# Layer normalisations applied on ScalarE as scale and shift, with the shift and three routing steps on GpSimd

## The chip, the cores and the metric

The kernel runs on one core of a Trainium2 chip. The metric is device time in microseconds (us) of one execution. The engines are named as in the profile: PE (TensorE matmul), PEld (its weight load), DVE (VectorE), ACT (ScalarE), POOL (GpSimd), SP (SyncE, which issues DMAs).

## What is computed

A decoder layer with three residual blocks, each followed by a layer normalisation without gain and bias. x is 16 batches of 256 rows of 256, ctx 16 x 77 x 256.

```
def _layernorm(x, axis=-1, eps=1e-05):
    m = jnp.mean(x, axis=axis, keepdims=True)
    v = jnp.var(x, axis=axis, keepdims=True)
    return (x - m) / jnp.sqrt(v + eps)

x = _layernorm(x + self_attention(x, W_qkv, W_out))        # 16 heads, segments of 128 queries, 64 keys each
x = _layernorm(x + cross_attention(x, ctx, Wq, Wk, Wv, Wo, biases))   # 16 heads, 77 keys
x = _layernorm(x + moe(x))
# moe: logits = x @ router_w; expert = argmax(logits); weight = softmax(logits)[expert]
#      weight * (gelu(x @ w1[expert] + b1[expert]) @ w2[expert] + b2[expert]), 14 experts
```

## The kernel before

Everything is fp32. **Part 1** (up to about 500 us) does the two attentions, their normalisations and the routing, batch by batch. **Part 2** sorts the rows by expert through a list in DRAM and runs 45 tiles of 128 rows through the experts; the change doesn't touch it.

Part 1 is a software pipeline of 21 iterations. In iteration i every engine runs through its own table of jobs, PE_ORDER, ACT_ORDER, DVE_ORDER, POOL_ORDER, in the order written there. An entry such as `ln11@2` is job ln, part 11, on batch i - 2. An entry whose batch is outside 0 to 15 is left out. Within an engine nothing overtakes: an instruction that waits holds all behind it. The tables have six rows; row n belongs to softmax unit n. Units 0 and 1 are the two segments of self-attention (1024 columns), units 2 to 5 the four parts of cross-attention (616 columns).

For a unit: PE `scores` (L556, L565) into the banks ps_s; DVE `max` (L934), `less_max` (L945); ACT `exp` (L812); DVE `sum` (L953), `reciprocal` (L965); POOL `scale` (L1210); PE `probT` (two transposes into PSUM, L543); ACT copies each (L792); PE `attend` (L598, L610); ACT `take_o` (L800, L805).

All other results of PE go through the four banks of ps_r. The jobs of PE that use them follow each other as a ring, so each job takes the bank of the job four places earlier and waits until that one has been emptied (`wait_bank`). In row 4 of PE_ORDER the ring goes probT20, probT21, k0, rk0, oa1, q0: **oa1 takes the bank of probT20, and q0 that of probT21**; in row 5 probT30 takes that of rk0.

Each batch has four normalisations of 128 x 256: 10 and 11 after self-attention (halves 0 and 1 of x1), 20 and 21 after cross-attention (x2s). For each, PE projects (`oa0`, `oa1`, `ox0`, `ox1`, L622), DVE adds the residual into a sum (L986), then bn_stats (L993) and bn_aggr (L1002) for mean and variance; POOL adds eps (L1197) and takes the power -0.5 (L1199); DVE subtracts the mean and multiplies by rstd (L1020, `ln`). x1 goes to PE's x1T and the query projection, x2s to x2T, to DRAM and to the router.

The routing of a batch is 12 small DVE operations (`r_max` to `r_place`, 128 x 28 or less), chained on one semaphore: maximum, logits less maximum (L1042, for ACT's exp of the gate), is-maximum, first of them, counts of earlier rows (L1054, L1058), one-hot. PE `rk` turns them into ranks, which DVE copies out of PSUM (L972), masks (`r_pick`, L1069) and sums (`r_place`, L1072). POOL `enter` writes two entries of the batch into the list by indirect DMA (L1286); the next batch's `r_gate` (L1066) waits until these have landed.

Of the kernel before, what the change touches and what calls it, by code (L numbers as in the profile page):

```python
# [6 lines left out]
P = 128  # L7
# [3 lines left out]
ALU = mybir.AluOpType  # L11
# [25 lines left out]
def decoder_layer(nc, x, x_cols, xk_cols, ctx_cols, w_qkv, w_out, wq, bq, wk, bk, wv, bv, wo, bo, router_w, w1, b1, w2,  # L37
# [31 lines left out]
    with ExitStack() as top:  # L69
# [54 lines left out]
        with ExitStack() as part1:  # L124
# [33 lines left out]
            rstd = sb1("rstd", [P, 4])  # L158
            x1 = sb1("x1", [P, TPB, D])
# [17 lines left out]
        with ExitStack() as part2:  # L177
            def sb2(name, shape, dt=F32):
# [59 lines left out]
        taken = {j: signal(f"taken_{j}", n) for j, n in JN.items()}  # L238
# [42 lines left out]
        def exists(b):  # L281
# [21 lines left out]
            sum0@1 r_weigh0@5 reciprocal0@1 max1@1 r_first0@5 less_max1@1 ln20@3 once0@1  # L303
            sum1@1 r_count0@5 reciprocal1@1 max2@2 less_max2@2 r_onehot0@5 ox1@3 stats21@3 mean21@3
            sum2@2 r_count_tile0@5 reciprocal2@2 max3@2 less_max3@2 r_gate_sum0@5 oa0@1 stats10@1 mean10@1
            sum3@2 reciprocal3@2 ln10@1 max4@2 less_max4@2 r_gate0@5 rk0@5 oa1@1 stats11@1 mean11@1
            ln21@3 sum4@2 r_pick0@5 reciprocal4@2 max5@2 less_max5@2 r_place0@5
# [37 lines left out]
        def wait_bank(pe, what, part, b):  # L345
# [269 lines left out]
        def pe_job(pe, job, part, b):  # L615
# [64 lines left out]
            elif job == "rk":  # L680
                pe.wait_ge(routed.sem, routed.at(b, STAGES.index("count_tile")))
# [133 lines left out]
        def act_take(act, job, part, b):  # L815
# [37 lines left out]
            elif job == "rt":  # L853
                wait(act, routed, b - 1, STAGES.index("is_max"))
                last = nc.scalar.copy(logits[:], src[:, 0:TPB * RW].rearrange("p (t e) -> p t e", t=TPB)[:, :, 0:E])
            last.then_inc(taken[job].sem, 1)

        def act_gate_exp(act, b):
# [3 lines left out]
            act.wait_ge(routed.sem, routed.at(b, STAGES.index("less_max")))  # L862
            wait(act, routed, b - 1, STAGES.index("gate_sum"))
# [8 lines left out]
        def act_iteration(act, i):  # L872
            for what, k, lag in in_order(ACT_ORDER):
# [93 lines left out]
        def dve_take(dve, job, part, b):  # L967
# [3 lines left out]
            if job == "rk":  # L971
                nc.vector.tensor_copy(rank[:], src[:, 0:TPB * E].rearrange("p (t e) -> p t e", t=TPB)).then_inc(  # L972
                    taken[job].sem, 1)
                return
# [438 lines left out]
```

## Time and profile before

| | |
|---|---|
| three runs | 716.0, 716.43 (median), 716.88 us |
| the profiled execution | 715.96 us, span of its trace 714.2 us |
| PE busy in the span | 601.3 us (84%) |
| DVE busy | 499.4 us (70%) |
| ACT busy | 347.7 us (49%) |
| POOL busy | 399.3 us (56%) |

In a timeline row stand start, duration, engine, line, operation, out<-in with shapes, how often, and in brackets the engine's idle time before it with what ended it. A row of the chain of waits has start, duration and what the end of the program waited for at that time. A row of busy times by stretch has the stretch, its length, the busy us of PE, PEld, DVE, ACT and POOL (with instruction counts), the granted TensorE clock as a share of full speed, the DMA share and GB/s. A row of one source line has the smallest, median and largest duration in ns. PE is pipelined, so a busy PE is not a PE at its peak.

### The profile page before, as it was taken

Reading aid. Unit: us, or ns where it says so; the run is one execution under the profiler, and the core shown is the slowest. Engines: PE = TensorE matmul, PEld = TensorE weight load, DVE = VectorE, ACT = ScalarE, POOL = GpSimd, SP = SyncE. Lnnn points to the kernel's source line nnn. Section 1 sums busy time; section 2 is a strip of 40 time slices with the busy share of each in tenths; the row PEclk is TensorE's granted clock in tenths of the full one; section 3 lists DMA queues with packets and bytes.
Section 4 is the critical chain, followed back from the end, with each engine's and each line's share of the span. In section 5 each row is a group of like instructions: output and inputs, shape, how many; then the busy total and the mean of one; then the engine's idle time right before and its main releaser. Section 6 shows DMA issues by size and latency. Waiting matters only on the chain.

```text
span 714.2 us, 17657 instructions
## 1 busy us (share of the span) xinstructions
PE 601.3 (84%) x5736; PEld 493.6 (69%) x5736; DVE 499.4 (70%) x1186; ACT 347.7 (49%) x864; POOL 399.3 (56%) x517
## 2 busy tenths in 40 slices
PE   4679889889898898898988988867279999999991
PEld 3457667667676676676766766645149999999991
DVE  2468868887898798887988878764305556655662
ACT  1346555555555555555555645533034554455540
POOL 3334645655575566564755655534334777777753
PEclk9889999999999999999999999987579999999996
DMA  8223133032231330331313101000033333333200
GB/s 275 83 58 92 21 112 110 13 112 78 53 111 32 101 109 14 112 106 26 111 34 98 29 12 32 18 20 16 1 70 77 100 93 90 97 89 106 72 28 1
DMA packets 75882, 50.17 MB, mean 70 GB/s; under 512 B 38918, under 2 KB 69898, under 8 KB 75792
## 3 DMA queue, kind: packets, MB, share of 16 engines
q1 hardware_dynamic: 70448, 40.60, 20.7%
q0 software_dynamic: 5344, 8.44, 4.0%
q8 instruction: 48, 0.79, 0.5%
q14 instruction: 42, 0.34, 0.2%
HBM read 40.54 MB, written 10.60 MB: 72 GB/s over the span
## 4 chain that ended last, share of the span: by engine, by line
PE 40%; POOL 17%; DVE 17%; issue 16%; ACT 5%; DMA 3%; SPq 1%; POOLq 0%; DVEq 0%; ACTq 0%
PE ps_r L622 17%; PE ps_r L543 7%; POOL out L1359 7%; POOL xg L1347 6%; DVE prob L945 5%; DVE mx L934 5%; PE ps_r L610 4%; PE ps_s L565 3%; POOL rs L1367 3%; DVE den L953 3%; ACT prob L812 3%; PE ps_r L652 2%; DMA token_lists<-member,place_i 2%; ACT qxT L848 2%; PE ps_r L670 2%
## 5 line engine op out<-in xcount | busy, mean ns | idle before, releaser
L1210 POOL TENSOR_TENSOR prob<-prob,rden 128x616 f32<-128x616 f32 (+1 forms) x96 | 138.6, 1444 | 160.5 <-DVE rden L965 160.3
L812 ACT ACTIVATE prob<-prob 128x616 f32<-128x616 f32 (+1 forms) x96 | 80.0, 833 | 68.7 <-DVE prob L945 68.7
L953 DVE TENSOR_REDUCE den<-prob 128x8 f32<-128x616 f32 (+1 forms) x96 | 88.7, 924 | 28.2 <-ACT prob L812 28.2
L934 DVE TENSOR_REDUCE mx<-ps_s 128x8 f32<-128x616 f32 (+1 forms) x96 | 87.0, 907 | 25.1 <-PE ps_s L556 22.3
L792 ACT COPY probT<-ps_r 128x512 f32<-128x512 f32 x192 | 83.3, 482 | 32.0 <-PE ps_r L543 32.0
L543 PE MATMUL ps_r<-ident,prob 128*128 128x128 f32 (+1 forms) x576 | 89.8, 296 | 2.7 <-POOL prob L1210 2.7
L945 DVE TENSOR_TENSOR prob<-ps_s,mx 128x616 f32<-128x616 f32 (+1 forms) x96 | 90.2, 940 | 2.5
L757 PEld LDWEIGHTS ps_s<-xgT,w1b 128*128 128x128 f32 x720 | 87.7, 193 | 6.1 <-ACT xgT L899 3.8
L909 ACT ACTIVATE hT<-ps_s,b1t 128x128 f32<-128x128 f32 x180 | 51.7, 368 | 81.3 <-PE ps_s L757 81.2
L757 PE MATMUL ps_s<-xgT,w1b 128*128 128x128 f32 x720 | 88.6, 277 | 3.1 <-ACT xgT L899 3.1
L769 PE MATMUL ps_r<-w2s,hT 128*128 x360 | 85.9, 382 | 0.0
L543 PEld LDWEIGHTS ps_r<-ident,prob 128*128 128x128 f32 (+1 forms) x576 | 65.1, 146 | 22.7 <-issue 22.6
L565 PE MATMUL ps_s<-kxblk,qxT 32*128 32x154 f32 x512 | 35.3, 345 | 44.4 <-ACT qxT L848 28.7
L769 PEld LDWEIGHTS ps_r<-w2s,hT 128*128 128x128 f32 x360 | 65.6, 192 | 7.4 <-issue 0.2
L565 PEld LDWEIGHTS ps_s<-kxblk,qxT 32*128 32x128 f32 x512 | 20.7, 185 | 67.3 <-issue 45.6
L1161 DVE TENSOR_TENSOR yb<-ps_r,b2r 128x256 f32<-128x256 f32 x45 | 19.1, 425 | 60.2 <-PE ps_r L769 60.2
L1347 POOL DMA_INDIRECT xg<-x_rows,slots x45 | 47.4, 1053 | 15.5 <-issue 9.4
L1359 POOL DMA_INDIRECT out<-yo,slots x45 | 47.9, 1064 | 13.1 <-issue 13.1
L1367 POOL TENSOR_TENSOR rs<-ve,neg_half 128x1 f32<-128x1 f32 x45 | 25.3, 562 | 38.2 <-DVE ve L1182 38.2
L1286 POOL DMA_INDIRECT token_lists<-member,place_i x32 | 32.8, 1026 | 21.6 <-DVE place_i L1072 13.9
L610 PE MATMUL ps_r<-probT,vX 128*32 128x128 f32 (+1 forms) x1024 | 42.7, 285 | 1.1 <-ACT probT L792 1.1
L622 PE MATMUL ps_r<-x1T,wT 128*128 128x256 f32 x128 | 32.8, 401 | 7.8 <-ACT x1T L835 7.8
(141 smaller groups left out, 1096.1 us busy)
## 6 DMA issues: line engine op xcount, KB each, us to landing
w1s<-in_w SPq DMA_DIRECT2D x14, 512.0 KB
w2s<-in_w SPq DMA_DIRECT2D x14, 512.0 KB
b2r<-in_b SPq DMA_DIRECT2D x45, 128.0 KB, 3.1
xT<-in_x_cols SPq DMA_DIRECT2D x16, 256.0 KB, 3.3
xres<-in_x SPq DMA_DIRECT2D x16, 256.0 KB, 4.4
x_rows<-x2s SPq DMA_DIRECT2D x32, 128.0 KB, 1.9
xkT<-in_xk_cols SPq DMA_DIRECT2D x16, 128.0 KB, 3.7
ctxT<-in_ctx_cols SPq DMA_DIRECT2D x16, 77.0 KB, 4.8
```

What stands on the lines that cost most here:

```text
L543: return nc.tensor.transpose(dst, src, ident[:])
L622: last = nc.tensor.matmul(dst[:, 0:width], lhs(c), rhs(c), start=(c == 0), stop=(c == KC - 1))
L757: last = nc.tensor.matmul(ps_s[:, m % 2, u * P:(u + 1) * P], w1b[:, m % 2, c, u * P:(u + 1) * P], xgT[:, m % 2, c * P:(c + 1) * P], start= ...
L769: last = nc.tensor.matmul(ps_r[:, (m - 1) % 2, 0:D], hT[:, (m - 1) % 2, c, :], w2s[:, bass.ds(e_before, 1), c, :].rearrange("p a f -> p (a ...
L792: nc.scalar.copy(probT[0:rows, par, first:last], src[0:rows, 0:last - first]).then_inc(pT_copied[kind].sem, 1)
L812: nc.scalar.activation(prob[:, n % 3, 0:width], prob[:, n % 3, 0:width], ACT.Exp, scale=SCALE).then_inc(exp_done[kind].sem, 1)
L934: nc.vector.tensor_reduce(m, s, axis=AX, op=ALU.max).then_inc(max_done[kind].sem, 1)
L945: nc.vector.tensor_tensor(p, s, mb, ALU.subtract).then_inc(sub_done[kind].sem, 1)
L953: nc.vector.tensor_reduce(den[:, par, 0:heads], prob[:, n % 3, 0:heads * width].rearrange("p (h k) -> p h k", k=width), axis=AX, op=ALU.ad ...
L1210: nc.gpsimd.tensor_tensor(p, p, rden[:, par, 0:heads, None].to_broadcast([P, heads, width]), ALU.mult).then_inc(scaled[kind].sem, 1)
L1347: nc.gpsimd.indirect_dma_start(xg[:, m, :], None, x2_dram, bass.IndirectOffsetOnAxis(ap=slots_no[:, j, 0:1], axis=0), bounds_check=B * S - ...
L1359: nc.gpsimd.indirect_dma_start(out_rows, bass.IndirectOffsetOnAxis(ap=slots_no[:, j - 4, 0:1], axis=0), yo[:, r, :], None, bounds_check=B ...
```

## The change

DVE's four `ln` operations per batch go to ACT, as `Identity(sum * rstd + shift)`; scale and bias are operands of 128 x 1. POOL makes `shift = (0 - mean) * rstd` with two more operations per normalisation. DVE's less_max, count and count_tile of the routing go to POOL. The copy of the ranks out of PSUM is dropped: `r_pick` reads them there, and PE's next user of that bank waits for r_pick. Each routing stage has a semaphore of its own. PE_ORDER, SP_ORDER and the order of all other entries stay.

```diff
         ACT_ORDER = """
-            kx0@2 take_o3@3 probT40@3 probT41@3 vx0@2 exp0@1 once0@1
+            kx0@2 take_o3@3 probT40@3 probT41@3 ln11@2 vx0@2 exp0@1 once0@1
...
-            take_o5@3 probT00@1 probT01@1 exp2@2 rt0@4
+            take_o5@3 probT00@1 probT01@1 ln20@3 exp2@2 rt0@4
...
-            take_o1@1 probT20@2 probT21@2 k0@0 exp4@2 q0@0
-            take_o2@2 probT30@2 probT31@2 exp5@2 v0@0
+            take_o1@1 ln10@1 probT20@2 probT21@2 k0@0 exp4@2 q0@0
+            take_o2@2 ln21@3 probT30@2 probT31@2 exp5@2 v0@0
...
         DVE_ORDER = """
-            sum5@3 r_max0@5 reciprocal5@3 max0@1 r_less_max0@5 r_is_max0@5 less_max0@1 ln11@2 ox0@3 stats20@3 mean20@3
+            sum5@3 r_max0@5 reciprocal5@3 max0@1 r_is_max0@5 less_max0@1 ox0@3 stats20@3 mean20@3
...
         POOL_ORDER = """
-            rstd11@2 scale5@3
-            rstd20@3 scale0@1 kxblk0@2
-            scale1@1
+            rstd11@2 scale5@3 r_less_max0@5
+            rstd20@3 scale0@1 kxblk0@2 r_count0@5
+            scale1@1 r_count_tile0@5
...
+        def act_layernorm(act, which, k, b):
+            q = 2 * (which - 1) + k
+            act.wait_ge(shift_done[which].sem, shift_done[which].at(b, k))
...
+            nc.scalar.activation(dst[:, k, :], sums(which, k)[:], ACT.Identity, bias=shift[:, q:q + 1],
+                                 scale=rstd[:, q:q + 1]).then_inc(ln_done[which].sem, 1)
...
             elif stage == "pick":
-                dve.wait_ge(taken["rk"].sem, taken["rk"].at(b))
-                last = nc.vector.tensor_tensor(rank[:], rank[:], hot, ALU.mult)
+                wait(dve, computed["rk"], b)
+                ranks = bank_of("rk", "0", b)[:, 0:TPB * E].rearrange("p (t e) -> p t e", t=TPB)
+                last = nc.vector.tensor_tensor(rank[:], ranks, hot, ALU.mult)
...
         def pool_rstd(pool, which, k, b):
...
+            nc.gpsimd.tensor_tensor(less_mean[:, q:q + 1], zeros[:, 0:1], mv[:, q, 0:1], ALU.subtract)
             nc.gpsimd.tensor_tensor(ve[:, q:q + 1], mv[:, q, 1:2], eps[:], ALU.add).then_inc(eps_added[which].sem, 1)
             pool.wait_ge(eps_added[which].sem, eps_added[which].at(b, k))
             nc.gpsimd.tensor_tensor(rstd[:, q:q + 1], ve[:, q:q + 1], neg_half[:], ALU.pow).then_inc(
                 rstd_done[which].sem, 1)
+            pool.wait_ge(rstd_done[which].sem, rstd_done[which].at(b, k))
+            nc.gpsimd.tensor_tensor(shift[:, q:q + 1], less_mean[:, q:q + 1], rstd[:, q:q + 1], ALU.mult).then_inc(
+                shift_done[which].sem, 1)
```

ACT in row 4 of a full iteration, before: the copies of probT20 (128x512) and probT21 (104x128) stand right behind take_o1 (oTa). In square brackets stand the semaphores that an instruction waits for.

```order
L800 COPY oTa<-ps_r 128x2x128 [waits computed_oa,pv_done_a]
L792 COPY probT<-ps_r 128x512 [waits pv_done_a,pT_done_x]
L792 COPY probT<-ps_r 104x128 [waits pT_done_x]
L823 COPY kT<-ps_r 128x256 [waits kblk_made,computed_k]
L812 ACTIVATE prob<-prob 128x616 [waits sub_done_x]
```

The same rows after:

```order
L808 COPY oTa<-ps_r 128x2x128 [waits computed_oa,pv_done_a]
L878 ACTIVATE x<-sum,shift,rstd 128x256 [waits x1r_made,computed_x1T,shift_done1]
L800 COPY probT<-ps_r 128x512 [waits pv_done_a,pT_done_x]
L800 COPY probT<-ps_r 104x128 [waits pT_done_x]
L831 COPY kT<-ps_r 128x256 [waits kblk_made,computed_k]
L820 ACTIVATE prob<-prob 128x616 [waits sub_done_x]
```

ln10 now stands between take_o1 and the copies, with a wait for the shift. In rows 5 and 0 ln21 stands in the same way ahead of the copies of probT30, and ln11 ahead of vrow (vx0) and exp0; in row 2 ln20 stands behind the copies of probT0, ahead of exp2.

PE in row 4, after: k0, rk0 (onehot, before), then oa1 (wout_s) and q0 (xT). These rows stand as they did before, but for `routed` in place of `routed_count_tile`.

```order
L630 MATMUL ps_r<-xkT,wqkv_s 128x128 x3
L690 MATMUL ps_r<-onehot,tri 128x64 [waits routed_count_tile,o_taken_a]
L691 MATMUL ps_r<-before,ones 128x64
L630 MATMUL ps_r<-wout_s,oTa 128x256 [waits o_taken_a,pT_copied_x]
L630 MATMUL ps_r<-wout_s,oTa 128x256
L630 MATMUL ps_r<-xT,wqkv_s 128x256 [waits x_loaded0,pT_copied_x]
```

Nothing moved here, and the wait of oa1 for pT_copied_x is the copy of probT20.

POOL from x1r in row 3 to scale3 in row 4, before (rstd10, then rstd21):

```order
L1230 TENSOR_TENSOR x1r<-x,bo_s 128x512 [waits taken_ox,ln_done1]
L1197 TENSOR_TENSOR ve<-mv,eps 128x1 [waits mean_done1]
L1199 TENSOR_TENSOR rstd<-ve,neg_half 128x1 [waits eps_added1]
L1197 TENSOR_TENSOR ve<-mv,eps 128x1 [waits mean_done2]
L1199 TENSOR_TENSOR rstd<-ve,neg_half 128x1 [waits eps_added2]
L1210 TENSOR_TENSOR prob<-prob,rden 128x616 [waits rec_done_x]
```

And after:

```order
L1238 TENSOR_TENSOR x1r<-x,bo_s 128x512 [waits taken_ox,ln_done1]
L1186 TENSOR_TENSOR less_mean<-zeros,mv 128x1 [waits ln_done1,mean_done1]
L1187 TENSOR_TENSOR ve<-mv,eps 128x1
L1189 TENSOR_TENSOR rstd<-ve,neg_half 128x1 [waits eps_added1]
L1192 TENSOR_TENSOR shift<-less_mean,rstd 128x1 [waits rstd_done1]
L1186 TENSOR_TENSOR less_mean<-zeros,mv 128x1 [waits ln_done2,mean_done2]
L1187 TENSOR_TENSOR ve<-mv,eps 128x1
L1189 TENSOR_TENSOR rstd<-ve,neg_half 128x1 [waits eps_added2]
L1192 TENSOR_TENSOR shift<-less_mean,rstd 128x1 [waits rstd_done2]
L1218 TENSOR_TENSOR prob<-prob,rden 128x616 [waits rec_done_x]
```

Each group has two operations more; `less_mean` is its first, and `shift`, behind a wait for the power, its last.

## Rows read from the trace of the kernel before

**Rows 1.** Busy time of each engine in one full iteration

```profile
249.83:277.74 27.91, 24.85 (x288) 19.53 (x289) 24.25 (x54) 15.97 (x37) 17.04 (x22) 1.00 0.26 73
```

**Rows 2.** Chain of waits through that iteration: start, us, what

```profile
249.83 0.44 DVE sum2b L986
...
253.40 0.54 PE ps_s L565 x8
...
265.78 0.88 PE ps_r L670 x4
...
266.94 1.06 ACT prob L812
...
277.74 0.44 DVE sum2b L986
```

**Rows 3.** Longest wait of PE there: us in total, times, longest

```profile
PE ps_s L565 <- ACT qxT L848: 1.9, 1, 1.9
```

**Rows 4.** DVE's ln (L1020) in the iteration, and one removed routing operation

```profile
249.83:277.74 27.91, 2.03 (x4) 1.00 0.26 73
...
L1058 DVE TENSOR_TENSOR before<-before,onehot x16: 140/164/173, 136.6 to 505.8; 128x14 f32<-128x14 f32 x16
```

**Rows 5.** Timeline of row 4, around normalisation 10 and oa1

```profile
254.26 0.18 DVE L1002 BATCH_NORM_AGGREGATE mv<-st 128x2 f32<-128x6 f32 x1
...
254.53 0.19 POOL L1197 TENSOR_TENSOR ve<-mv,eps 128x1 f32<-128x1 f32 x1
...
254.80 0.55 POOL L1199 TENSOR_TENSOR rstd<-ve,neg_half 128x1 f32<-128x1 f32 x1
...
255.14 0.76 ACT L792 COPY probT<-ps_r 128x512 f32<-128x512 f32 x2 [0.18 <-PE ps_r L543]
...
255.31 0.19 POOL L1197 TENSOR_TENSOR ve<-mv,eps 128x1 f32<-128x1 f32 x1
...
256.28 0.73 PEld L622 LDWEIGHTS ps_r<-wout_s,oTa 128*128 128x128 f32 x4
```

**Rows 6.** Groups of ACT by shape, 184 to 240 us: busy us, mean ns

```profile
L792 ACT COPY probT<-ps_r 128x512 f32<-128x512 f32 x16 | 9.0, 588 | 2.8 <-PE ps_r L543 2.8
...
L792 ACT COPY probT<-ps_r 104x128 f32<-104x128 f32 x8 | 2.2, 272 | 0.0
...
L848 ACT ACTIVATE qxT<-ps_r,bq_s 128x256 f32<-128x256 f32 x4 | 1.6, 461 | 0.0
L800 ACT COPY oTa<-ps_r 128x256 f32<-128x256 f32 x4 | 1.5, 373 | 4.0 <-PE ps_r L598 4.0
```

**Rows 7.** Timeline: the same place in iterations 3 and 16

```profile
83.76 0.75 ACT L792 COPY probT<-ps_r 128x512 f32<-128x512 f32 x2 [0.18 <-PE ps_r L543]
...
84.45 0.73 PEld L622 LDWEIGHTS ps_r<-wout_s,oTa 128*128 128x128 f32 x4
...
454.41 0.73 PEld L622 LDWEIGHTS ps_r<-wout_s,oTa 128*128 128x128 f32 x4 [0.25 <-ACT probT L792]
```

**Rows 8.** Timeline of row 0: rstd11 on POOL and vx0 on ACT

```profile
264.91 0.57 POOL L1199 TENSOR_TENSOR rstd<-ve,neg_half 128x1 f32<-128x1 f32 x1
...
266.68 0.37 ACT L839 COPY vrow<-ps_r 77x256 f32<-77x256 f32 x1 [1.10 <-PE ps_r L670]
```

**Rows 9.** The clock: the chain's iteration before, and one stretch of 10 us

```profile
220.28 0.44 DVE sum2b L986
...
410.00:420.00 10.00, 7.61 (x57) 6.40 (x56) 7.15 (x13) 5.42 (x12) 4.60 (x4) 0.83 0.10 14
```

**Rows 10.** Timeline of the end of part 1: the last three list entries

```profile
495.62 0.18 DVE L1072 TENSOR_REDUCE place_i<-rank 128x2 uint32<-128x28 f32 x1
...
496.60 1.06 POOL L1286 DMA_INDIRECT token_lists<-member,place_i  x1 [1.45 <-DVE ismax L1045]
...
503.08 0.17 DVE L1066 RECIPROCAL member<-lsum 128x2 f32<-128x2 f32 x1 [5.19 <-DMA token_lists<-member,place_i]
...
503.66 0.18 DVE L1072 TENSOR_REDUCE place_i<-rank 128x2 uint32<-128x28 f32 x1
```

More of the change, by code:

```diff
@@ L158, in decoder_layer @@
             rstd = sb1("rstd", [P, 4])
+            less_mean = sb1("less_mean", [P, 4])
+            shift = sb1("shift", [P, 4])
             x1 = sb1("x1", [P, TPB, D])
@@ L244, in decoder_layer @@
         eps_added = {n: signal(f"eps_added{n}", 2) for n in (1, 2)}
+        shift_done = {n: signal(f"shift_done{n}", 2) for n in (1, 2)}
         rstd_done = {n: signal(f"rstd_done{n}", 2) for n in (1, 2)}
         ln_done = {n: signal(f"ln_done{n}", 2) for n in (1, 2)}
-        STAGES = ("max", "less_max", "is_max", "weigh", "first", "count", "onehot", "count_tile", "gate_sum", "gate",
-                  "pick", "place")
-        routed = signal("routed", len(STAGES))
+        ROUTE_DVE = ("max", "is_max", "weigh", "first", "onehot", "gate_sum", "gate", "pick", "place")
+        ROUTE_POOL = ("less_max", "count", "count_tile")
+        routed = {stage: signal(f"routed_{stage}", 1) for stage in ROUTE_DVE + ROUTE_POOL}
         gate_exp_done = signal("gate_exp_done", 1)
@@ L293, in decoder_layer @@
         ACT_ORDER = """
[L294 removed]
+            kx0@2 take_o3@3 probT40@3 probT41@3 ln11@2 vx0@2 exp0@1 once0@1
             take_o4@3 gate_exp0@5 probT50@3 probT51@3 x1T0@2 x2T0@4 exp1@1 qx0@2
[L296 removed]
+            take_o5@3 probT00@1 probT01@1 ln20@3 exp2@2 rt0@4
             take_o0@1 probT10@1 probT11@1 exp3@2
[L298 to L299 removed]
+            take_o1@1 ln10@1 probT20@2 probT21@2 k0@0 exp4@2 q0@0
+            take_o2@2 ln21@3 probT30@2 probT31@2 exp5@2 v0@0
         """
         DVE_ORDER = """
[L302 to L307 removed]
+            sum5@3 r_max0@5 reciprocal5@3 max0@1 r_is_max0@5 less_max0@1 ox0@3 stats20@3 mean20@3
+            sum0@1 r_weigh0@5 reciprocal0@1 max1@1 r_first0@5 less_max1@1 once0@1
+            sum1@1 r_onehot0@5 reciprocal1@1 max2@2 less_max2@2 ox1@3 stats21@3 mean21@3
+            sum2@2 reciprocal2@2 max3@2 less_max3@2 r_gate_sum0@5 oa0@1 stats10@1 mean10@1
+            sum3@2 reciprocal3@2 max4@2 less_max4@2 r_gate0@5 oa1@1 stats11@1 mean11@1
+            sum4@2 r_pick0@5 reciprocal4@2 max5@2 less_max5@2 r_place0@5
         """
         POOL_ORDER = """
[L310 to L312 removed]
+            rstd11@2 scale5@3 r_less_max0@5
+            rstd20@3 scale0@1 kxblk0@2 r_count0@5
+            scale1@1 r_count_tile0@5
             scale2@2 x1r0@2
@@ L359, in wait_bank @@
                 wait(pe, o_taken[kind], at_b, k)
+            elif name == "rk":
+                wait(pe, routed["pick"], it - lag)
             else:
@@ L384, in wait_for, with sums @@
                 wait(eng, signals[event[0]], event[2], event[1])
+        def sums(which, k):
+            return ((sum1, sum1b), (sum2, sum2b))[which - 1][k]
         block = top.enter_context(nc.Block())
@@ L970, in dve_take @@
             dve.wait_ge(computed[job].sem, computed[job].at(b, k))
[L971 to L974, printed above, removed]
             which = 1 if job == "oa" else 2
             s = sums(which, k)
+            wait(dve, ln_done[which], b - 1, k)
             if job == "oa":
@@ L1128, in link @@
                 dve.wait_ge(dve2.sem, chain[0])
-            dve.wait_ge(routed.sem, routed.at(B - 1))
+            wait(dve, routed["count_tile"], B - 1)
+            wait(dve, routed["place"], B - 1)
             dve.wait_ge(total_done.sem, 1)
@@ L1266, in pool_iteration @@
                     pool_enter(pool, b)
+                elif what[:2] == "r_":
+                    pool_route(pool, what[2:], b)
                 else:
@@ L1283, in pool_enter @@
                 if t == 0:
-                    pool.wait_ge(routed.sem, routed.at(b))
+                    wait(pool, routed["place"], b)
+                    wait(pool, routed["gate"], b)
                     pool.wait_ge(token_stepped.sem, token_stepped.at(b))
```

97 lines of the change are left out of this document (48 added, 49 removed).

## The prediction

> **What bounds the kernel now.** I read the busy time of a full iteration first. Of 27.91 us PE is busy for 24.85 and DVE for 24.25 [rows 1], so neither share says which of them decides, and both have idle time. The chain of waits says it. It goes round once per iteration through the same four pieces [rows 2]: DVE from the addition behind ox1 (249.83) to less_max3; PE without a gap from scores4 (253.40) to vx0 (265.78 + 0.88 = 266.66), through k0, rk0, oa1 and q0; then in turns ACT exp0 (266.94), DVE sum0, max1 and less_max1, ACT exp1 and the copy qx0; then PE from scores2 to ox1, which releases the DVE again (277.74). The waits of PE agree: the longest is 1.9 us, for qx0 [rows 3], and between scores4 and vx0 there is none. So a DVE instruction is on the path only if it stands in the first or the third piece, and anything that delays one of PE's jobs from scores4 to vx0 costs the whole of it, once per iteration.
>
> **What is removed: from DVE.** The four ln take 2.03 us of DVE per iteration [rows 4]; the three routing steps and the rank copy are four operations of about 0.165 us, 0.66 us [rows 4]. That is 2.7 us of busy time per batch. What of it is on the path? ln10 and ln21 stand in rows 4 and 5, beside PE's unbroken piece; ln11 stands behind less_max0, where ACT's exp0 waits for vx0 of PE and not for DVE; ln20 stands behind less_max1, before sum1, which waits for exp1. The routing steps lie in the gaps that DVE leaves between an operation and the next that needs its result. I take 0 for all of it in the steady state; the cover is PE's piece and the two exponentials, and if it were gone each of these would count in full.
>
> **What is added: the shift, on POOL and ACT.** Row 4 decides [rows 5]. Before, mean10 ends at 254.26 + 0.18 = 254.44; POOL starts eps at 254.53, 0.09 later, the power at 254.80, and ends it at 255.35. With less_mean ahead and shift behind: less_mean at 254.53; eps at 254.68 (POOL starts an independent operation 0.04 before the last one ends: 255.31 against 255.35); the power 0.27 after that, 254.95 to 255.50; shift 0.08 behind it, as the power stands behind eps, 255.58 to 255.77. ACT sees that 0.09 later: ln10 starts at 255.85. No ACTIVATE from SBUF with both operands per partition is in the trace. One with a bias from PSUM takes 0.461 us, a plain copy of the same size 0.373 [rows 6]; a second such operand may cost nothing or those 0.09 again, so 0.46 to 0.55. ACT starts an independent instruction 0.10 before the last one ends (0.588 + 0.272 against the pair's 0.76) [rows 5, 6]. So probT20's copy starts at 256.21 to 256.30 instead of 255.14, and ends 0.59 later, at 256.80 to 256.89.
>
> The Trainium skill (ScalarE: Activation LUTs, What ACT_TABLE_LOAD costs) gives 186 ns + 0.833 ns per element, and about 93 ns more for each operand of this kind: 585 ns here, and my estimate from it would be the upper end of what I took. For the copies with one such operand it gives 492 ns where the row has 461. Its rules for kernel authors (same page) send additions and multiplications to VectorE; the rows agree that ACT isn't quicker at this, but that is not what costs here.
>
> **Who waits for that copy.** oa1 takes the bank of probT20. Before, the copy ended at 255.14 + 0.59 = 255.73 and PE came to oa1 at 256.28 [rows 5], 0.46 us after it could have started. Now PE can start it at 256.89 to 256.98: **PE stands 0.61 to 0.70 us, I take 0.65**, in its unbroken piece, with q0, scores5 and everything up to vx0 behind it. In iterations 2 to 4 there is no rk0 and PE comes to oa1 just when the copy is done (83.76 + 0.59 = 84.35, PE at 84.45) [rows 7]: the whole shift of the copy counts, 1.07 to 1.16, I take 1.1. In iteration 16 there are no k0 and q0, and PE already waits 0.25 us there [rows 7]; DVE, which comes next on the path, had some slack, but POOL's longer rstd11 then stands ahead of scale5, on which PE waits; I take 0.8 between 0.5 and 1.2. In iteration 1 probT20 doesn't exist: 0. Sum: 3 x 1.1 + 11 x 0.65 + 0.8 = **+11.25 us**. Bounds: 3 x 1.0 + 11 x 0.5 + 0.5 = 9 and 3 x 1.25 + 11 x 0.8 + 1.2 = 13.8, the ends of the ranges above and 0.1 us for waits that take longer or shorter on another engine.
>
> **The other three ln and the routing.** ln11 on ACT stands ahead of vx0 and exp0. The power ends at 264.91 + 0.57 = 265.48 and PE frees ACT's vrow at 266.68 [rows 8]. The two added operations make the shift 0.42 later, 265.90; ln11 runs from 265.99 to 266.54, and lets the next start at 266.44: 0.24 us before vrow could. Cost 0; the cover is thin. ln21 delays the copies of probT30 by less than 0.1, and no job of PE needs those banks before row 0. ln20 delays exp2 by 0.46; its sum2 stands behind the addition of ox1, more than 1 us later. ln20 is done before SP, busy with place_v, comes to store_x0; store_x1 issues some 2 us later, and SP's next loads are for the next iteration. less_max, count and count_tile on POOL (about 0.2 us each) stand where POOL waits for a reciprocal. probT30 now waits for r_pick, which stands 0.4 us or more ahead. All 0.
>
> **The end of part 1.** After 495 us the chain is place, two list DMAs, gate, rank copy, pick, place, once per batch. The place of batch 13 (495.62) stood behind rank copy and ln21, themselves behind count_tile, which waited for the ox1 addition; it can come about 1.1 us earlier, but POOL's longer rstd21 holds the DMA (496.60) back: between 0.3 and 1.0, I take 0.6. In the two rounds after it, gate at 503.08 to place at 503.66 is 0.58 us [rows 10] and loses the rank copy: 0.25 each. Together **-1.1 us** (-0.8 to -1.5).
>
> **TensorE's clock.** Between 100 and 450 us the granted clock is 1.00 but for five stretches of 10 us with 0.83, at 100, 160, 240, 330 and 410, of which the last stands in [rows 9]: in a part of each it was 1.2 GHz. The fall comes after the stand of 1.9 us before scores2 [rows 3], which every iteration has, but from 160 on in one iteration of three only. Such an iteration is longer: 220.28 to 249.83 is 29.55 us [rows 9], the next 27.91 [rows 1], 1.64 us per fall. Which iterations fall is a matter of how that stand lies in time, and the change lengthens every iteration by 0.65 us. By these stretches one fall came 60 to 90 us after the other. Two iterations of 28.56 and a fall are 58.8 us, three are 87.3; a fall in every second instead of every third is what I hold likeliest, three more: **+4.9 us**. Bounds: one fewer (-1.6), seven more (+11.5).
>
> **Sum.** The profiled execution took 715.96 us, its span being 714.2; the median of the runs, 716.43, is 0.07% above it. 715.96 + 11.25 - 1.1 + 4.9 = **731.0 us**.
>
> **Rivals.** (a) The stall comes, but the clock falls as often as before: 731.0 - 4.9 = 726.1. For it: the stand before scores2 is unchanged, and the new one of 0.65 is short. (b) ln11 is later than worked out by 0.5 us or more; it then holds vx0 and exp0 too, on the path: 0.3 us x 16 = 4.8 and one fall more, 1.6: 737.4. For it: the cover of 0.24 us; against it: where the path moves later, POOL has the same time. (c) **Faster.** The relief of DVE reaches the path and the stall doesn't come. If shift10 is ready 0.65 us earlier than worked out, oa1 never waits; then DVE's pieces, whose every step stands behind a wait, lose 0.2 us in each of 16 iterations (one routing operation each time), 3.2, the end loses 1.1, and a fall fewer takes 1.6: 715.96 - 5.9 = 710.1. For it: DVE's 24.25 us of 27.91, less 2.7. Against it: the power alone takes 0.55 of the way to 255.35, and less_mean and shift can't come for nothing. (d) Both effects small, the copy 0.5 us late and oa1's slack used up, the rest lost in the end's gain: 716.
>
> **Chances.** Forecast 0.55, (a) 0.25, (b) 0.08, (c) 0.07, (d) 0.05. The range reaches from (a) with the low bound of the stall and one fall fewer, 715.96 + 9 - 1.5 - 1.6 = 721.9, to (b), with the forecast's upper part 715.96 + 13.8 - 0.8 + 9.8 = 738.8: 722 to 739. About 0.2%, 1.4 us, is what can be told from no change. Faster 0.07, within 0.2% 0.04, slower 0.89.
>
> **What would show it.** Right: PE waits some 0.65 us for ACT's probT copy before oa1 in iterations 5 to 15, and 1.1 in 2 to 4; ACT's ln10 waits for POOL's shift; iterations of about 28.55 us where the clock is full; DVE's busy time down by some 40 us and its idle time up by more; more stretches at a clock of 0.83. The end of part 1 after 495 us shorter by 1 us; part 2 as it was. Wrong: oa1 without a wait; full iterations of 27.9 us or less; vrow behind ln11. I would be wrong most of all if PE's second weight load had reached oa1 later than before for another reason, or if the falls of the clock did not follow the length of the iteration.

## The result, and the profile after

The changed kernel takes **736.18 us** (median of four runs, 734.89 to 739.16), the kernel before beside it 716.65: a ratio of **1.0268**, 95% interval 1.0222 to 1.0314. It is slower. The forecast was 731.0, in a range of 722 to 739. The profiled execution took 736.03 us, with a span of 734.3, 20.1 more than before.

The top of the page after (busy us, share of the span, instructions; in the order PE, PEld, DVE, ACT, POOL):

```profile
span 734.3 us, 17942 instructions
...
PE 612.7 (83%) x5736; PEld 504.5 (69%) x5736; DVE 458.1 (62%) x1058; ACT 375.5 (51%) x928; POOL 427.6 (58%) x693
```

DVE has 41 us less to do than before and the kernel is 20 us longer. The same view as [rows 1]: a full iteration in which the clock stays full and one in which it falls, and then ACT's ln (L878) alone in the first of them:

```profile
200.49:229.03 28.54, 25.07 (x288) 19.61 (x289) 21.76 (x46) 17.67 (x41) 18.77 (x33) 1.00 0.27 71
...
229.03:259.15 30.12, 26.65 (x288) 21.01 (x288) 21.74 (x45) 17.85 (x42) 18.75 (x33) 0.94 0.37 73
```

```profile
200.49:229.03 28.54, 2.42 (x4) 1.00 0.27 71
```

The iteration went from 27.91 to 28.54 us, and DVE's 24.25 us in it to 21.76. A fall of the clock, a stretch in which the granted clock goes from 1.00 to half, still costs 1.6 us (30.12 against 28.54).

Row 4 of that iteration in the timeline, against [rows 5]:

```profile
204.06 0.54 PE L573 MATMUL ps_s<-kxblk,qxT 32*128 32x154 f32 x8 [0.67 <-DVE prob L970]
...
204.93 0.18 DVE L1024 BATCH_NORM_AGGREGATE mv<-st 128x2 f32<-128x6 f32 x1
205.19 0.19 POOL L1186 TENSOR_TENSOR less_mean<-zeros,mv 128x1 f32<-128x1 f32 x1 [0.15 <-DVE mv L1024]
205.33 0.19 POOL L1187 TENSOR_TENSOR ve<-mv,eps 128x1 f32<-128x1 f32 x1
205.60 0.56 POOL L1189 TENSOR_TENSOR rstd<-ve,neg_half 128x1 f32<-128x1 f32 x1
...
206.23 0.19 POOL L1192 TENSOR_TENSOR shift<-less_mean,rstd 128x1 f32<-128x1 f32 x1
...
206.46 0.60 ACT L878 ACTIVATE x<-sum,shift,rstd 128x256 f32<-128x256 f32 x1 [0.83 <-POOL shift L1192]
...
206.96 0.73 ACT L800 COPY probT<-ps_r 128x512 f32<-128x512 f32 x2
...
207.58 1.13 PE L630 MATMUL ps_r<-wout_s,oTa 128*128 128x256 f32 x4 [0.41 <-ACT probT L800]
```

ACT waits 0.83 us for POOL's shift, ln10 takes 0.60, and only then comes the copy of probT20, for which PE now stands (waits without work) before oa1. From scores4 to the first weights of oa1 PE takes 3.52 us (204.06 to 207.58, where weights and matmul start together), before 2.88 (253.40 [rows 2] to 256.28 [rows 5]): 0.64 us. The bracket shows 0.41 of it, counted from the modelled end of the matmul before. The chain of waits now goes through the added work: start, us, what.

```profile
204.93 0.19 DVE mv L1024
...
205.60 0.56 POOL rstd L1189
...
206.23 0.20 POOL shift L1192
...
206.96 0.57 ACT probT L800
...
207.58 1.56 PE ps_r L630 x6
```

Three of the waits over the whole program, not the longest ones: what waited, for whom, us in total, times, longest. The first counts every job of L630 that waits for a copy of probT, not oa1 alone.

```profile
PEld ps_r L630 <- ACT probT L800: 20.5, 30, 1.4
ACT x L878 <- POOL shift L1192: 20.2, 28, 2.5
DVE onehot L1047 <- POOL before L1204: 12.1, 4, 4.1
```

The third is DVE's one-hot behind POOL's count, four times, from 486.87 us on, where the pipeline drains. f1 below has the same waits and loses nothing at its end.

**Where the 20.1 us are.** The additions behind ox1 (`sum2b`) mark the iterations; a period is the time from one to the next. The first starts 3.2 us later than before (81.62 against 78.45). From there to the fourteenth it is 385.36 us against 370.01, 15.35 more. The next period gives 0.7 more, the last one 0.2 less. From the last addition to the last pair of list entries it is 19.21 against 20.00 us, 0.8 less, and from there to the end 203.0 against 201.2, 1.8 more. The 15.35 us are 11 periods with 0.64 more, two (iterations 3 and 4) with 1.07 and 0.99, and four more falls of the clock: nine instead of five. One of the stretches of 10 us with a fall after:

```profile
190.00:200.00 10.00, 7.61 (x57) 6.39 (x55) 5.98 (x11) 5.75 (x13) 4.95 (x6) 0.83 0.13 21
```

### The profile page after: what moved, and what is told of

Its sections match the earlier page's. It is cut to its first block, busy times and chain, and to the rows that moved or that the text cites. A ratio compares the mean times of both kernels' runs of the same rounds, so it can differ in the third digit from the quotient of the medians.

```text
span 734.3 us, 17942 instructions
## 1 busy us (share of the span) xinstructions
PE 612.7 (83%) x5736; PEld 504.5 (69%) x5736; DVE 458.1 (62%) x1058; ACT 375.5 (51%) x928; POOL 427.6 (58%) x693
## 4 chain that ended last, share of the span: by engine, by line
PE 49%; DVE 16%; issue 14%; POOL 10%; ACT 6%; DMA 4%; SPq 0%; POOLq 0%; ACTq 0%; DVEq 0%
PE ps_r L630 15%; PE ps_s L765 8%; PE ps_r L551 7%; PE ps_r L777 7%; DVE mx L959 5%; PE ps_r L618 4%; DVE prob L970 3%; DVE den L978 3%; ACT prob L820 3%; POOL out L1370 2%; PE ps_s L573 2%; PE ps_r L660 2%; DMA token_lists<-member,place_i 2%; DVE st L1014 2%; PE ps_r L678 2%
## 5 line engine op out<-in xcount | busy, mean ns | idle before, releaser
L551 PE MATMUL ps_r<-ident,prob 128*128 128x128 f32 (+1 forms) x576 | 95.6, 309 | 3.1 <-POOL prob L1218 2.1
L765 PEld LDWEIGHTS ps_s<-xgT,w1b 128*128 128x128 f32 x720 | 89.9, 197 | 6.5 <-ACT xgT L924 4.3
L765 PE MATMUL ps_s<-xgT,w1b 128*128 128x128 f32 x720 | 91.1, 281 | 3.1 <-ACT xgT L924 3.1
L551 PEld LDWEIGHTS ps_r<-ident,prob 128*128 128x128 f32 (+1 forms) x576 | 69.8, 154 | 23.8 <-issue 22.1
L630 PE MATMUL ps_r<-wout_s,oTa 128*128 128x256 f32 x128 | 35.1, 398 | 8.1 <-ACT probT L800 8.1
```

The costliest lines, as they stand in the source:

```text
L551: return nc.tensor.transpose(dst, src, ident[:])
L630: last = nc.tensor.matmul(dst[:, 0:width], lhs(c), rhs(c), start=(c == 0), stop=(c == KC - 1))
L765: last = nc.tensor.matmul(ps_s[:, m % 2, u * P:(u + 1) * P], w1b[:, m % 2, c, u * P:(u + 1) * P], xgT[:, m % 2, c * P:(c + 1) * P], start= ...
```

## The experiments

The theory: ln10 ahead of probT20's copy makes PE stand before oa1, and a longer iteration makes the clock fall more often. Rivals: the load of ACT as such; the routing or POOL's extra work; falls that come from another part of the change.

The experiments ran on two chips, and this has to be kept apart. In the first and third group (e1 to e4, e5 to e8) the kernel before took 744.37 and 746.36 us on its chip; in the second group (f0 to f4) 716.88 us, as in the result above. I call them the 744 chip and the 716 chip. Ratios are always against the kernel before on the same chip. The second group is the one that explains the result, so it comes first.

### On the 716 chip

**f0**, the kernel before:

> The kernel before the change, unchanged, for its trace beside those of the experiments on the same chip. In the first four experiments the kernel before took 744.4 us and not 716.4 on their chip, and DVE's max0 waited 1.7 us for PE's scores0 in nine of nine iterations, which neither of the first two traces shows. If this is such a chip: time about 744, the wait of max0 for scores0 is there too, and by the theory that falls of the clock follow the length of the iteration they account for the rest: iterations near 28.8 us without a fall, and a fall in most of them. If it is a chip like that of the first two traces: 716 to 717 us, and the five falls again.

716.36 us, ratio 1.0009 (0.9987 to 1.0032), the same five falls. It is the reference for the three below.

**f1**, the changed kernel with ln10 behind the copies:

```diff
-            take_o1@1 ln10@1 probT20@2 probT21@2 k0@0 exp4@2 q0@0
+            take_o1@1 probT20@2 probT21@2 ln10@1 k0@0 exp4@2 q0@0
```

> The changed kernel with ln10 behind the copies of probT20 and probT21, once more. On a chip where the kernel before takes 716 us: by the theory of the stall 27.9 us per iteration, no wait of oa1, five falls, 715 to 719 us; if the load of ACT is what costs, 28.5 us and 734 to 737; if falls come from POOL or the routing, 27.9 us with eight or nine falls, 722 to 725. On a chip like the last one: 735 us again.

717.75 us, ratio **1.0007** (0.9985 to 1.0030). One entry moved by two places gives the whole loss back. ACT's ln and POOL's shift are all still there. A full iteration, and its row 4 (ACT's copy, then ln10, PE's weights for oa1):

```profile
194.08:221.98 27.90, 24.84 (x288) 19.52 (x288) 21.75 (x45) 17.83 (x42) 18.79 (x33) 1.00 0.31 77
```

```profile
197.65 0.54 PE L573 MATMUL ps_s<-kxblk,qxT 32*128 32x154 f32 x8 [0.67 <-DVE prob L970]
...
199.39 0.75 ACT L800 COPY probT<-ps_r 128x512 f32<-128x512 f32 x2 [0.18 <-PE ps_r L551]
...
200.04 0.60 ACT L878 ACTIVATE x<-sum,shift,rstd 128x256 f32<-128x256 f32 x1
...
200.53 0.73 PEld L630 LDWEIGHTS ps_r<-wout_s,oTa 128*128 128x128 f32 x4
```

2.88 us from scores4 to oa1, no wait, 27.90 us per iteration, five falls. The load of ACT is no cause, nor is the routing. It also says what the 41 us taken from DVE are worth here: nothing that can be measured.

**f4**, the kernel before with spare work on ACT. Nothing of the change is in it:

```diff
-            take_o1@1 probT20@2 probT21@2 k0@0 exp4@2 q0@0
+            take_o1@1 spare0@2 probT20@2 probT21@2 k0@0 exp4@2 q0@0
...
+                elif what == "spare":
+                    for m in range(2):
+                        nc.scalar.copy(spare_out[:, m, :], spare_in[:])
```

> The kernel before with two spare ACT copies of 128 x 735 ahead of probT20's copy, once more. On a chip where the kernel before takes 716 us: by the theory of the stall and of falls that follow the length of the iteration, 28.5 us per iteration, eight or nine falls, 732 to 736 us; with falls from another cause, 28.5 us and five or six falls, 725 to 728; if the loss has nothing to do with the copy, 716 to 718. On a chip like the last one: 747 us again.

734.45 us, ratio **1.0243** (1.0198 to 1.0289). Row 4, and two iterations, without and with a fall:

```profile
203.45 1.51 ACT L890 COPY spare_out<-spare_in 128x735 f32<-128x735 f32 x2
...
204.87 0.75 ACT L794 COPY probT<-ps_r 128x512 f32<-128x512 f32 x2
...
205.50 1.13 PE L624 MATMUL ps_r<-wout_s,oTa 128*128 128x256 f32 x4 [0.41 <-ACT probT L794]
```

```profile
198.43:226.95 28.52, 25.06 (x288) 19.60 (x289) 24.27 (x54) 17.16 (x39) 17.06 (x22) 1.00 0.25 72
...
226.95:257.07 30.12, 26.65 (x288) 21.01 (x289) 24.27 (x54) 17.37 (x39) 17.07 (x22) 0.94 0.28 77
```

The same wait of 0.41 us, the same period (28.52 against 28.54) and nine falls, in the same iterations as in the changed kernel. Here DVE has its 24.27 us and POOL its 17.07. A late copy alone makes the loss, and at this equal length, on this chip, the falls are the same whatever made the iteration longer.

**f2**, the changed kernel:

> The changed kernel, unchanged, beside the three others on one chip. On a chip where the kernel before takes 716 us: 735 to 737, nine falls, iterations of 28.54 us without a fall. On a chip like the last one: by the theory of the stall 0.6 to 0.7 us more per iteration than with ln10 behind the copies, so 29.8 to 29.9 us, and 743 to 747 us if the clock falls as seldom as there.

735.24 us, ratio 1.0257 (1.0216 to 1.0297). The profiled execution, at 738.91, was above that median and had ten falls, two of them twice as long as the others; its iterations without one are 28.53 us. So one program, or one period, doesn't always have the same number of falls.

### On the 744 chip

**e1**, the same edit as f1:

> The changed kernel with one entry of ACT's table moved: ln10 stands behind the copies of probT20 and probT21 instead of ahead of them. All else of the change stays (DVE's ln on ACT, the two more POOL operations, the routing on POOL). Theory of the prediction (the stall of oa1 behind the late copy makes the loss, and the longer iteration makes more clock falls): oa1 no longer waits for probT20's copy, 2.88 us from scores4 to oa1 instead of 3.52; iterations of 27.9 us where the clock is full; clock falls as before the change (5 instead of 9 between iterations 3 and 16); 715 to 719 us. Rival 1 (the load of ACT by four operations of 0.60 us is what costs, wherever they stand): ACT has the same work, so iterations stay at 28.5 us, 734 to 737. Rival 2 (clock falls come from another part of the change, for instance POOL or the routing): iterations of 27.9 us but 8 or 9 falls, 722 to 725.

735.16 us, ratio **0.9865** (0.9820 to 0.9911). The number looks like Rival 1, and means something else: on this chip the kernel before isn't at 716 but at 744.37. Against it the changed kernel with ln10 moved is *faster*. What differs on the chip shows where DVE's max0 waits for PE's scores0:

```profile
268.27 0.73 PE L564 MATMUL ps_s<-kblk,qT 32*128 32x128 f32 x16
...
270.41 1.23 DVE L959 TENSOR_REDUCE mx<-ps_s 128x16 f32<-128x1024 f32 x1 [1.69 <-PE ps_s L564]
```

By the modelled end scores0 is done at 269.00; its result comes at 270.41, 1.4 us later. That wait is there nine times out of nine between 170 and 430 us in e1, e2, e3 and e4. It isn't in the iterations before the first list entries (0.34 us at 123.07 in e1), and the one from 109.66 takes 27.46 us, as in f0. With it a full iteration is 29.2 us instead of 27.9:

```profile
255.20:284.39 29.19, 25.13 (x288) 19.52 (x288) 22.43 (x45) 17.77 (x42) 18.76 (x33) 1.00 0.27 75
```

**e2**, the routing part alone, ln on DVE as before. Two of the changed lines, against the changed kernel:

```diff
-            take_o1@1 ln10@1 probT20@2 probT21@2 k0@0 exp4@2 q0@0
+            take_o1@1 probT20@2 probT21@2 k0@0 exp4@2 q0@0
...
-            sum3@2 reciprocal3@2 max4@2 less_max4@2 r_gate0@5 oa1@1 stats11@1 mean11@1
+            sum3@2 reciprocal3@2 ln10@1 max4@2 less_max4@2 r_gate0@5 oa1@1 stats11@1 mean11@1
```

> The routing part of the change alone: less_max, count and count_tile on POOL, no copy of the ranks, one semaphore for each routing stage; the four normalisations are applied on DVE as before. Theory of the prediction (this part costs nothing in the steady state and gives about 0.25 us in each of the last two rounds of list entries): 715 to 717 us, iterations of 27.9 us, five falls of the clock. Rival (part of the loss is the routing's: DVE now waits for POOL's count before the one-hot): iterations longer than 28.0 us and 720 or more.

737.54 us, ratio 0.9898 (0.9840 to 0.9956), 28.94 us without a fall, three falls. On this chip it is no loss. The absolute numbers of the expectation don't hold on this chip.

**e3**, the normalisations alone, routing as before. POOL's rows, against the changed kernel:

```diff
-            rstd11@2 scale5@3 r_less_max0@5
-            rstd20@3 scale0@1 kxblk0@2 r_count0@5
-            scale1@1 r_count_tile0@5
+            rstd11@2 scale5@3
+            rstd20@3 scale0@1 kxblk0@2
+            scale1@1
```

> The normalisation part alone: ln10, ln11, ln20 and ln21 on ACT where the change puts them, shift on POOL; the routing is as before, on DVE, with its copy of the ranks. Theory of the prediction (the whole loss is this part's): 734 to 738 us, iterations of 28.5 us, oa1 waits for ACT's copy of probT20, nine falls of the clock. Rival (the loss is spread over both parts): 720 to 730.

746.77 us, ratio 1.0031 (1.0004 to 1.0059). Row 4 is that of the changed kernel again:

```profile
264.92 0.60 ACT L875 ACTIVATE x<-sum,shift,rstd 128x256 f32<-128x256 f32 x1 [0.83 <-POOL shift L1203]
265.42 0.73 ACT L798 COPY probT<-ps_r 128x512 f32<-128x512 f32 x2
266.04 1.13 PE L628 MATMUL ps_r<-wout_s,oTa 128*128 128x256 f32 x4 [0.41 <-ACT probT L798]
```

Its iterations take 30.05 us, 1.1 more than those of e2: 0.64 of it is the stall, which therefore belongs to this part; some 0.35 the DVE operation of the last section, and the rest isn't accounted for. But there is one fall only, at 107 us, and none after it.

**e4**, the same edit as f4:

> The kernel before the change, with two spare ACT copies of 128 x 735 (0.61 + 0.09 us each by the slope of the copies in the profile, 1.4 us together) ahead of the copy of probT20, from a tile and into a tile that nothing else uses. No wait, no POOL operation and no normalisation is moved. probT20's copy then starts about 1.1 us later, past the 0.46 us that oa1 had in hand, so that oa1 stands 0.6 to 0.7 us as in the changed kernel. Theory of the prediction (any delay of that copy past 0.46 us makes the loss, and the clock follows the length of the iteration): iterations of 28.5 us where the clock is full, eight or nine falls, 732 to 736 us. Rival 1 (the clock falls more often because of something else in the change): iterations of 28.5 us but five or six falls, 725 to 728. Rival 2 (the loss has nothing to do with this copy): 716 to 718.

746.58 us, ratio 1.0029 (0.9996 to 1.0062). Iterations of 29.77 us without a fall, three falls.

**e5 and e6**, f4's edit with another stall:

```diff
-            spare_in = sb1("spare_in", [P, 735])
+            spare_in = sb1("spare_in", [P, 540])
...
+            spare_in = sb1("spare_in", [P, 590])
...
+                    for m in range(3):
```

The first is e5 (two copies of 128 x 540), the other two lines are e6 (three of 128 x 590).

> The kernel before with two spare ACT copies of 128 x 540 ahead of probT20's copy, 1.08 us together where two of 128 x 735 (1.40 us) gave a full iteration of 28.52 us instead of 27.90. So oa1 should stand 0.3 us: full iterations of 28.2 us. Theory that the falls of the clock follow the length of the iteration, in proportion between 5 at 27.90 and 9 at 28.52: about 7 falls in the thirteen periods from iteration 3 on; 11 x 0.3 + 3 x 0.75 + 0.4 = 5.9 us of stall and 2 x 1.64 = 3.3 us of falls, 725 to 727 us. Rival 1 (a stand before oa1 of any length brings four more falls): 728 to 730. Rival 2 (only a stand above some length brings falls): five falls, 722 to 723.

> The kernel before with three spare ACT copies of 128 x 590 ahead of probT20's copy, 1.74 us together: oa1 should stand 0.96 us, full iterations of 28.86 us. Theory that falls follow the length of the iteration in proportion: about 11 falls in thirteen periods; 11 x 0.96 + 3 x 1.4 + 1.0 = 15.8 us of stall and 6 x 1.64 = 9.8 us of falls, 740 to 744 us. Rival 1 (four more falls whatever the stand): 738 to 740. Rival 2 (no dependence, five falls): 731 to 733.

743.65 us, ratio 0.9981 (0.9945 to 1.0016), and 754.97 us, ratio 1.0126 (1.0060 to 1.0193). A full iteration without a fall of each:

```profile
229.19:258.65 29.46, 25.35 (x288) 19.61 (x289) 24.30 (x54) 16.92 (x39) 17.07 (x22) 1.00 0.27 74
```

```profile
235.48:265.59 30.11, 25.35 (x288) 19.60 (x289) 24.34 (x54) 17.47 (x40) 17.07 (x22) 1.00 0.26 73
```

The size of the stall is confirmed: spare work of 1.08, 1.40 and 1.74 us gives iterations of 29.46, 29.77 and 30.11, one for one. The dependence of the falls on the length isn't what I expected. The count in the thirteen periods from the first addition behind ox1 to the fourteenth:

| kernel | chip | period without a fall | falls |
|---|---|---|---|
| before, f0, f1 | 716 | 27.90 | 5, 5, 5 |
| after, f4, f2 | 716 | 28.54, 28.52, 28.53 | 9, 9, 10 |
| e8, e7 | 744 | 28.61, 28.86 | 0, 0 |
| e2, e1 | 744 | 28.94, 29.19 | 3, 2 |
| e5, e4 | 744 | 29.46, 29.77 | 4, 3 |
| e3, e6 | 744 | 30.05, 30.11 | 1, 6 |

"In proportion to the length" is wrong. On the 716 chip equal periods gave equal falls, but for the ten of f2; on the other, 30.05 us had one and 30.11 us six. What the counts go with there is how long PE stands before scores2. Every fall in the table begins 0.4 to 1.7 us behind the start of scores2. Once the list entries are there, that stand is 1.55 to 1.56 us in e1 and e3, and 1.65 in e2, e4, e5 and e6. In e3 and in e6:

```profile
315.10 0.54 PE L571 MATMUL ps_s<-kxblk,qxT 32*128 32x154 f32 x8 [1.55 <-ACT qxT L854]
```

```profile
323.51 0.54 PE L567 MATMUL ps_s<-kxblk,qxT 32*128 32x154 f32 x8 [1.65 <-ACT qxT L850]
```

Of the 20 stands of 1.56 us in those periods none is followed by a fall, of the 40 of 1.65 us ten are. Of the stands of 1.95 us it is 9 of 18 on this chip (before the list entries) and 43 of 78 on the 716 chip, where all are that long. Which ones among stands of equal length are followed by a fall may be a matter of how they lie in time. That is argued and not shown: no run moved the stand in time and left its length. And in e1 and e3 other things differ too (ln stands on ACT and POOL has more to do); only the swap of e7 and e8 was made to shorten the stand.

The kernel before is as slow as e3 on the 744 chip though nothing delays its oa1. No trace of it from that chip was taken, but the clock of its runs speaks for more falls: its 19 executions had a mean granted clock of 0.929 to 0.941, the ten of e3 beside them 0.948 to 0.955 and the ten of e4 0.941 to 0.950. The median one, 742.7 us at 0.934, was at half clock for 98 us by my estimate (742.7 x 0.066 x 2), where the eight traces of that chip give 61 to 88 us. How many falls these are, and where, stays open. So a ratio against the kernel before on that chip mixes shorter periods with fewer falls.

**e7 and e8**, qx0 ahead of exp1 on ACT, in the kernel before and in f1's kernel:

```diff
-            take_o4@3 gate_exp0@5 probT50@3 probT51@3 x1T0@2 x2T0@4 exp1@1 qx0@2
+            take_o4@3 gate_exp0@5 probT50@3 probT51@3 x1T0@2 x2T0@4 qx0@2 exp1@1
```

> The kernel before with two entries of ACT's table swapped: the copy qx0 ahead of exp1 in row 1. PE's stand before scores2 ends with qx0; the projection that qx0 copies is done at 271.85 in the iteration from 249.83, exp1 starts at 271.91 and qx0 at 272.87. Ahead of it qx0 starts at 271.9: the stand falls from 1.9 to about 0.95 us, and exp1 is 0.8 us later, which comes back in part through sum1 and exp2, so that an iteration is 0.7 us shorter: 27.2 us. Theory that the falls come from this stand where it lies in time so that they can: a stand half as long brings none from 160 us on; 716.5 - 14 x 0.7 - 5 x 1.64 = 698 us (695 to 702). Rival 1 (the falls do not come from this stand): 27.2 us but as many falls, 706 to 708. Rival 2 (exp1's delay holds probT1 or exp2 by as much as is gained): 714 to 718.

> The changed kernel with ln10 behind the copies of probT20 and probT21, and with the same swap of qx0 and exp1 on ACT: a candidate to beat both kernels. If the relief of DVE is worth nothing, as the prediction has it: as the kernel before with the swap, 698 us (695 to 702), no falls from 160 on. Rival 1 (with exp1 later DVE comes onto the path, where it now has 2.7 us less to do): iterations 0.2 to 0.4 us shorter than those of the kernel before with the swap, 692 to 696. Rival 2 (nothing is gained): 714 to 718.

725.54 us, ratio **0.9734** (0.9670 to 0.9797), and 723.02 us, ratio **0.9696** (0.9632 to 0.9760). PE's stand before scores2, in e1 and in e8:

```profile
280.45 0.54 PE L573 MATMUL ps_s<-kxblk,qxT 32*128 32x154 f32 x8 [1.56 <-ACT qxT L856]
```

```profile
270.83 0.84 ACT L856 ACTIVATE qxT<-ps_r,bq_s 128x256 f32<-128x256 f32 x2 [1.66 <-PE ps_r L630]
271.56 1.05 ACT L820 ACTIVATE prob<-prob 128x1024 f32<-128x1024 f32 x1
271.77 0.54 PE L573 MATMUL ps_s<-kxblk,qxT 32*128 32x154 f32 x8 [0.98 <-ACT qxT L856]
...
247.11:275.71 28.60, 25.20 (x286) 19.52 (x286) 22.34 (x45) 17.88 (x42) 18.75 (x34) 1.00 0.27 76
```

The stand falls from 1.56 to 0.98 us and the iteration from 29.19 to 28.60; no fall comes in the thirteen periods of either kernel. e7 at 28.86 us has none where e2 at 28.94, with the longer stand, has three, all between 160 and 225 us. With the counts above that speaks for the stand as what the falls need; on the 716 chip it wasn't tried. In the first two periods, before the list entries, e7 takes 26.47 and 26.88 us where e2, also without a fall there, takes 27.47 twice. The gain, 20.8 and 23.3 us, is what was expected for the 716 chip (18.5 from 716.5 to 698), but there it wasn't run. With qx0 first, the rest of the change seems to be worth something: e8's median is 2.5 us below e7's, though their runs overlap, and its iteration 0.25 us shorter. e8 is 3.0% below the kernel before on that chip, 1.7% below e1, and 3.2% below e3, which has the changed kernel's stall; the changed kernel itself wasn't timed there.

## Why the prediction was right, and where not

**What bounds the kernel: right.** The claim was that whatever delays a job of PE between scores4 and vx0 costs the whole of it. e5, e4 and e6 show it one for one at oa1, the only job of the piece that was delayed.

**DVE's relief costs and gives nothing: right** in the steady state of the 716 chip (f1, 1.0007).

**The shift: right to 0.1 us.** Worked out were 1.77 to 1.86 us from the end of mean10 to the start of probT20's copy; it took 1.85 (205.11 to 206.96). Two of its pieces were off against each other: ACT started ln10 0.04 us behind the shift and not 0.09, and ln10 took 0.60 us and not 0.46 to 0.55. The rows of ACT had one operand per partition at most, and a source in PSUM; the step took the second operand to cost no more than the first, and was low by 0.05 to 0.14 us. The Trainium skill (ScalarE: Activation LUTs, What ACT_TABLE_LOAD costs) came to 585 ns by its rule, my estimate then; the trace has medians of 600 to 602, so its rule was nearer here than the rows I took.

**The stall: right.** Forecast 0.65, 1.1 and 0.8 us for iterations 5 to 15, 2 to 4 and 16, in all 11.25. Measured 0.64, about 1.05 (1.07 and 0.99 where it can be read) and 0.7: 10.9.

**ln11 and vrow: right, and thin.** vrow still waited for PE, 0.20 us, and not for ln11:

```profile
217.17 0.60 ACT L878 ACTIVATE x<-sum1b,shift,rstd 128x256 f32<-128x256 f32 x1 [0.30 <-POOL shift L1192]
...
217.97 0.37 ACT L847 COPY vrow<-ps_r 77x256 f32<-77x256 f32 x1 [0.20 <-PE ps_r L678]
```

**The end of part 1: about right.** Forecast -1.1; measured -0.2 in the last period and -0.8 behind it, -1.0. f1 has it too: 19.04 us from the last addition to the last pair of list entries, where f0 has 20.05. By steps: the first place came earlier but POOL's longer rstd21 held the DMA, as forecast, so that 3.45 us instead of 3.61 passed, a gain of 0.16 and not 0.6; of the two rounds behind it, forecast at 0.25 each, the first gave nothing (8.05 us, before 8.03) and the last 0.65. The sum came out by pieces that were off against each other.

```profile
515.50 1.06 POOL L1297 DMA_INDIRECT token_lists<-member,place_i  x1 [0.89 <-POOL member L1290]
```

**The clock: the term that was too small.** The step said "a fall in every second instead of every third", three more, +4.9 us. After 160 us there are two falls in three iterations, and four more in all: 4 x 1.6 = 6.4 us. The premise, that the falls follow the length of the iteration, holds between the two lengths of the 716 chip; on the 744 chip it doesn't, and the falls go with the length of PE's stand before scores2. The count was extrapolated from the distances between five falls, and e3 and e6 show how little such a count bears. Nor does its own rate give three: one fall in every second of thirteen periods makes six or seven, one or two more than five. Rival (a), no more falls, was 10 us short. The upper end of the range holds 9.8 us beside the stall that no step gives; with the clock's own bound of 11.5 it would have been 740.5, and the result lies inside either way.

**What was left out.** 3.9 us that stand in no step. The first addition behind ox1 came 3.2 us late, of which 1.1 is iteration 2's stall and 1.1 a longer wait for the first weights from DRAM; and part 2 took 1.8 us more. Neither is the change's: between two executions of the *same* kernel (before and f0) the first addition moved by 0.9 us and part 2 by 2.1 (201.2 and 199.1), and f4, which touches neither, has 202.3 for part 2. What differs is where the clock stands over the first tiles. After, and f0, from 530 us and 520 us:

```profile
530.00:540.00 10.00, 6.42 (x13) 3.39 (x14) 3.36 (x18) 0.62 (x1) 3.53 (x4) 0.61 0.01 1
540.00:550.00 10.00, 4.96 (x22) 3.75 (x20) 0.93 (x2) 2.54 (x5) 6.06 (x6) 0.83 0.35 87
550.00:560.00 10.00, 8.81 (x51) 8.45 (x52) 2.00 (x6) 4.83 (x17) 0.56 (x1) 0.83 0.32 77
```

```profile
520.00:530.00 10.00, 7.42 (x28) 3.96 (x26) 1.28 (x3) 2.07 (x3) 5.07 (x5) 0.84 0.27 68
530.00:540.00 10.00, 8.33 (x59) 7.91 (x60) 2.57 (x8) 5.97 (x19) 2.50 (x3) 1.00 0.34 82
```

f0 goes through its first tiles at full clock from 530 us on, the changed kernel goes through two more stretches at 0.83.

## What to carry to other kernels

Before work is moved to an idle engine, look at what stands behind it in that engine's order: ACT had half its time free, and an operation of 0.60 us with a wait ahead of it still cost 0.64 us per iteration, because a copy on which PE waits stood behind it. Two places further down the same work was free. And look for PE's longest stand in the loop: bringing it down to 0.98 us, by a swap of two entries of ACT's table, was worth 2.7% against the kernel before on the chip where it was tried, and 1.7% in e8 against e1, where both have a trace. No fall of the clock was left in the thirteen periods.

## What the runs showed of the hardware

**Chips differ.** The same kernel took 716.4 us on one chip and 744 to 746 on another. On the second PE's scores0 gives its result 1.4 us later than the records say, in every iteration with list entries, and part 2 takes 211 us (e1, from 523.82) where the traces of the first chip have 199 to 203. Why is open. The two chips rank kernels differently: f1 and the kernel before are equal on the one, and on the other e1 is 1.35% faster, beside a kernel before whose granted clock was lower there (0.934 against e1's 0.945 to 0.949).

**A small DVE operation can last as long as POOL's.** The first routing operation behind max0 (ismax, or ldif where that is still on DVE; 128 x 28) has a median of 177 to 178 ns on the 716 chip. On the 744 chip, where max0 ends later, POOL is already scaling when it starts, and it ends when POOL does. Its median there is 499 ns in e4 and 514 in e2, and 866 in e1 and 872 in e3, where POOL's two operations more put scale5 later. In e1 and in e2:

```profile
271.17 1.22 POOL L1218 TENSOR_TENSOR prob<-prob,rden 128x616 f32<-128x616 f32 x1
...
271.55 0.88 DVE L1035 TENSOR_TENSOR ismax<-logits,lmax 128x28 f32<-128x28 f32 x1
```

```profile
330.09 1.20 POOL L1233 TENSOR_TENSOR prob<-prob,rden 128x616 f32<-128x616 f32 x1
...
330.81 0.53 DVE L1049 TENSOR_TENSOR ismax<-logits,lmax 128x28 f32<-128x28 f32 x1
```

POOL ends at 272.39 and 331.29, ismax at 272.43 and 331.34. less_max0 stands behind it, on the path, and these 0.35 us cover the 0.25 by which e1's iteration is longer than e2's. So the two small POOL operations cost something on DVE there, and the records show it as a longer operation and not as a wait.

The Trainium skill (SBUF — State Buffer, SBUF: two separate sides) says of the port pair that DVE and GpSimd share that whichever operation starts first holds it for the whole instruction, and that a DVE operation with two SBUF inputs is one of those that are held up. ismax has two such inputs, and these rows agree.
